# Passage to attention: next batch's adapter first, maxima over two PSUM banks, rings on released rows, value products last, squares four a tile

## The chip, the cores and the metric

One Trainium2 chip, one of its cores, one program. The metric is the device time of one execution in microseconds, lower is better. Engines: PE multiplies matrices, ACT applies functions and copies, DVE does elementwise work and reductions, POOL (GpSimd) some elementwise work, SP issues most of the DMAs. Each has its own instruction stream and they meet through semaphores.

## The reference

`x` is 8 batches of 512 rows of 256. Four layers follow each other:

- L0, a quantised GELU-gated unit: `h = x * ((cond @ norm_w.T + 1) * rsqrt(mean(x*x) + eps))`, `val, gate = split(h @ up_w.T)`, `u = val * gelu(gate)`, u rounded to 8 bits per row, times ternary `down_w`, plus x. The mean square of each row of x is needed first: these are the squares of this case.
- L1, an adapter: `x + relu(x @ Wd_b.T + bd) @ Wu_b.T + bu`, with weights of its own for each batch, generated from `cond`.
- L2: `x + alpha * attention(gamma * rmsnorm(x) + beta)`, 16 heads of 16, softmax over 512 keys, then a SwiGLU unit of width 1024 in the same form.
- L3: layer norm, plus `tanh` of a condition, times weight, plus bias.

## The kernel before, in words

**L0** runs over 32 tiles of 128 rows (n = 0 to 31; four tiles are a batch). PE multiplies each for the gate half and the value half (`up`, L1383; 12 matmuls of 512 columns each, three passes for precision), transposes the quantised rows (`transpose_q`), multiplies by the down weights (`down`) and transposes back (`transpose_x1`). ACT does `gelu`, copies qT and x1T out of PSUM, and stores rounds of generated weights (`store_round`). Its `squares(n0, n1)` (L721) sums the squares of rows with an accumulator, `roots` takes the square root, DVE the reciprocal into `r0`. For tiles 8 to 31 this is done in two blocks of 12 squares behind tiles 5 and 6 (L943 to L948).

**L1 and attention** are a pipeline of steps `step(j, ..., i)`, i = 0 to 15, one for each head, in which batch a = j + 1 is in the adapter, p = j in the query, key and value products, b = j - 1 in attention, and f = j - 2 in the output product. Each engine has its own `step`, and the order of its work is written out by hand; there is no scheduler. `opening` and the tables `ACT_PLAN`, `DVE_PLAN`, `PE_PLAN` (L52) lay the steps of j = -1 and the first of j = 0 between the last tiles of L0. What is left of j = 0 stands behind the last tile: **the passage**.

Scores are computed twice. `max_scores` (L1462) multiplies 128 queries by the 512 keys of a head into one of two PSUM banks `mx_ps`, and DVE takes the maximum of each row (`take_maxima`, L1136); 16 such columns are a group of four heads (`turn_max` transposes them, POOL splits them, SP writes them to DRAM and reads them back as two extra rows of the query ring). The scores proper, `st_ps`, then already have the maximum taken off, ACT takes the exponential, and `av_ps` gathers weights times values. Maxima run `LEAD = 7` heads ahead, so the passage holds the maxima of heads 0 to 6 of batch 0 in its steps 9 to 15, and step 0 of the round j = 1 can begin with scores of head 0 and maxima of head 7.

Queries and keys go through DRAM into `qring` and `kring`, one slot for each group of four heads (`load_ring`, L467). The slots lie on the rows of SBUF that held the up weights, so the first load waits for the last value product of L0, `val_done` of NT = 32, and for the stores of both halves of queries and keys.

PSUM is shared: the two banks of `gate_ps` are later `mx_ps`, those of `val_ps` are `st_ps0`, that of x1T is `av_ps`, that of `gen_ps` is `misc`, in which all products of the adapter, of queries, keys and values stand one after another (`take_misc` waits for its last reader). `hf` holds the normalised rows of a batch: the value products (L1552) read it, the squares of the next batch's rows are written to it (L899), and POOL then writes the next batch's rows to it (L694).

## Time and profile before

| | us |
|---|---|
| median of 3 runs | 1108.82 (1108.29 to 1127.13) |
| profiled execution | 1111.15 |
| its span | 1108.5 |
| mean granted clock of PE | 0.971 of 2.4 GHz |
| PE busy | 1042.1 (94%) |
| DVE busy | 748.0 (67%) |
| ACT busy | 664.3 (60%) |
| POOL busy | 173.8 (16%) |
| chain that ended last: PE, DVE, ACT | 69%, 12%, 6% |

PE sets the length nearly everywhere, so the rows to look for are those in which PE waits, and who released it. Times in rows are from the span's start. In a row of the timeline the bracket gives how long the engine was idle before it and what ended that. A clock of 1.00 is 2.4 GHz, of 0.50 is 1.2 GHz.

### The profile page before, as it was taken

What the parts mean: (1) busy time and instruction counts of PE and PEld (TensorE: products, weight loads), DVE (VectorE), ACT (ScalarE), POOL (GpSimd) and SP (SyncE); (2) the same over time, 40 slices, a digit from 0 to 9 for tenths busy, and PEclk for the clock granted to TensorE, in tenths of its full rate; (3) what the DMA queues carried; (4) which work ended last, traced back from release to release, by engine and by line L of the source; (5) the groups of instructions that cost most, each with busy time, mean ns of one, the idle gap of its engine ahead of it and who ended that gap; (6) DMA issues with size and microseconds to landing.
All of it is one profiled execution on the core that took longest, in us unless ns stands there. A gap on an engine that the chain in (4) does not pass through costs nothing.

```text
span 1108.5 us, 16304 instructions
## 1 busy us (share of the span) xinstructions
PE 1042.1 (94%) x5286; PEld 637.4 (57%) x5286; DVE 748.0 (67%) x1211; ACT 664.3 (60%) x903; POOL 173.8 (16%) x203
## 2 busy tenths in 40 slices
PE   6989999999789999999999999999899999999996
PEld 4756767777535344343434344333268778787784
DVE  5755667787576777777776877778855565656654
ACT  5574334463335777878787777866763555555545
POOL 0000001120131132333232432221201000000000
PEclk9999999999958999999999999999999999999998
DMA  9924422002514355353635355354220000000001
GB/s 295 385 98 138 157 94 88 1 1 86 117 30 146 72 158 117 98 142 76 200 74 163 79 158 117 99 148 106 69 59 21 1 20 20 19 19 0 20 20 38
DMA packets 63576, 103.85 MB, mean 94 GB/s; under 512 B 18720, under 2 KB 28960, under 8 KB 62496
## 3 DMA queue, kind: packets, MB, share of 16 engines
q1 hardware_dynamic: 60784, 100.56, 31.0%
q10 hardware_dynamic: 2736, 2.57, 1.0%
q8 instruction: 32, 0.52, 0.2%
q14 instruction: 24, 0.20, 0.1%
HBM read 65.81 MB, written 33.03 MB: 89 GB/s over the span
## 4 chain that ended last, share of the span: by engine, by line
PE 69%; DVE 12%; issue 7%; ACT 6%; POOL 2%; DMA 2%; SPq 1%; ACTq 0%; DVEq 0%; POOLq 0%
PE st_ps L1635 13%; PE gate_ps L1392 8%; PE val_ps L1392 8%; PE mx_ps L1635 7%; PE st_ps L1522 7%; DVE mx L1142 6%; PE av_ps L1512 6%; PE misc_ps L1448 4%; PE mx_ps L1467 3%; PE misc_ps L1539 3%; PE y_ps L1402 3%; PE misc_ps L1552 2%; PE misc_ps L1543 1%; DVE stage L1152 1%; PE qT_ps L1410 1%
## 5 line engine op out<-in xcount | busy, mean ns | idle before, releaser
L1142 DVE TENSOR_REDUCE mx<-mx_ps 128x1 f32<-128x512 f32 x512 | 330.2, 685 | 132.0 <-PE mx_ps L1467 131.8
L1467 PE MATMUL mx_ps<-kring,qring 48*128 48x512 f32 x512 | 210.8, 477 | 14.5 <-DVE mx L1142 10.9
L1522 PE MATMUL st_ps<-qring,kring 50*128 50x512 f32 x512 | 190.6, 454 | 10.0 <-ACT shared L874 4.0
L1522 PEld LDWEIGHTS st_ps<-qring,kring 50*128 50x128 f32 x512 | 79.1, 189 | 161.5 <-issue 114.6
L874 ACT ACTIVATE pbuf<-st_ps 128x1024 f32<-128x1024 f32 x128 | 129.5, 1022 | 46.5 <-PE st_ps L1522 44.1
L874 ACT ACTIVATE shared<-st_ps 128x1024 f32<-128x1024 f32 x128 | 129.1, 1024 | 41.0 <-PE st_ps L1522 39.4
L1467 PEld LDWEIGHTS mx_ps<-kring,qring 48*128 48x128 f32 x512 | 89.2, 191 | 55.4 <-DVE mx L1142 51.8
L1294 DVE TENSOR_TENSOR shared<-st_ps,shared 128x512 f32<-128x512 f32 x64 | 44.2, 690 | 80.0 <-PE st_ps L1635 61.5
L991 ACT ACTIVATE p_hi<-shared 128x512 fp32r<-128x512 f32 x64 | 40.4, 631 | 71.1 <-DVE shared L1294 70.5
L1191 DVE SCALAR_TENSOR_TENSOR h<-val_ps,r,gelu 128x1024 f32<-128x1024 f32 x32 | 41.1, 1283 | 57.3 <-PE val_ps L1392 57.3
L1303 DVE TENSOR_TENSOR p_lo<-shared,p_hi 128x512 fp32r<-128x512 f32 x64 | 46.9, 733 | 37.7 <-ACT p_hi L991 37.0
L929 ACT ACTIVATE gelu<-gate_ps,r 128x1024 f32<-128x1024 f32 x32 | 35.7, 1116 | 57.7 <-PE gate_ps L1392 57.7
L1512 PE MATMUL av_ps<-shared,vaug 128*17 128x512 f32 x512 | 68.5, 607 | 1.5 <-ACT oaug L796 1.3
L975 ACT ACTIVATE shared<-mx_ps 128x512 f32<-128x512 f32 x64 | 38.2, 597 | 51.1 <-PE mx_ps L1635 51.0
L1512 PE MATMUL av_ps<-pbuf,vaug 128*17 128x512 f32 x512 | 66.8, 598 | 1.3 <-ACT oaug L796 1.1
L766 ACT ACTIVATE qT<-qT_ps 128x1024 bf16<-128x1024 bf16 x32 | 32.6, 1017 | 54.4 <-PE qT_ps L1410 50.8
L1392 PE MATMUL gate_ps<-up_hi,xs_lo 128*128 128x512 f32 x128 | 55.0, 430 | 6.9 <-DVE up_lo L1064 6.9
L1392 PE MATMUL val_ps<-up_hi,xs_lo 128*128 128x512 f32 x128 | 54.7, 427 | 0.0
L1392 PE MATMUL gate_ps<-up_lo,xs_hi 128*128 128x512 f32 x128 | 51.8, 405 | 0.0
L1392 PE MATMUL gate_ps<-up_hi,xs_hi 128*128 128x512 f32 x128 | 51.5, 403 | 0.0
L1392 PE MATMUL val_ps<-up_hi,xs_hi 128*128 128x512 f32 x128 | 51.3, 401 | 0.0
L1392 PE MATMUL val_ps<-up_lo,xs_hi 128*128 128x512 f32 x128 | 51.1, 400 | 0.0
(223 smaller groups left out, 2087.3 us busy)
## 6 DMA issues: line engine op xcount, KB each, us to landing
chunk<-in_gen_w SPq DMA_DIRECT2D x8, 2048.0 KB, 8.8
qring<-q_parts SPq DMA_DIRECT2D x64, 192.0 KB, 3.5
kring<-k_parts SPq DMA_DIRECT2D x64, 192.0 KB, 4.5
q_parts<-stage SPq DMA_DIRECT2D x16, 512.0 KB, 2.8
k_parts<-stage SPq DMA_DIRECT2D x16, 512.0 KB, 2.8
xres<-in_xT SPq DMA_DIRECT2D x8, 512.0 KB, 12.2
shared<-in_x SPq DMA_DIRECT2D x8, 512.0 KB, 12.1
q_parts<-stage SPq DMA_DIRECT2D x16, 256.0 KB, 3.0
```

What stands on the lines that cost most here:

```text
L874: nc.scalar.activation(pbuf[g % 2][:, i % GH, 2 * half:2 * half + 2], st_ps[half][:], ACT.Exp, scale=float(DH) ** -0.5).then_inc(S["exp"], 1)
L991: nc.scalar.activation(p_hi[f % 4][:], p_f, ACT.Copy).then_inc(F["p_hi"], 1)
L1142: nc.vector.tensor_reduce(mx[h // GH % 2][:, col:col + 1], mx_ps[qt % 2][:], AX, ALU.max).then_inc(S["mx_free"], 1)
L1191: nc.vector.scalar_tensor_tensor(out=h[:], in0=val_ps[:], scalar=r0[:, bass.ds(n, 1)], in1=gelu[:], op0=ALU.mult, op1=ALU.mult) \
L1294: nc.vector.tensor_tensor(p_f, fhid_ps[f % 2], silu[f % 2], ALU.mult) \
L1303: nc.vector.tensor_tensor(p_lo[f % 4][:], p_f, p_hi[f % 4][:].bitcast(F32), ALU.subtract) \
L1392: ins = nc.tensor.matmul(ps[:, half * 512:(half + 1) * 512], a[:, k, t * P:(t + 1) * P], w[:, k, o:o + 512], start=s == 0, stop=s == len(s ...
L1448: ins = nc.tensor.matmul(out, s(k), m(k), start=n == 0, stop=n == len(steps) - 1)
L1467: nc.tensor.matmul(mx_ps[qt % 2][:], qring[r:r + QROWS, h // GH, h % GH // 2, qt * P:(qt + 1) * P], kring[r:r + QROWS, h // GH, h % GH // ...
L1512: ins = nc.tensor.matmul(av_ps[32 * c:32 * c + DH + 1, :], vaug[:, kt, GH * vg + c, :], pbuf[vg % 2][:, c, kt, :], start=kt == 0, stop=kt ...
L1522: ins = nc.tensor.matmul(st_ps[half][:, kt % 2], kring[r:r + SROWS, g, i % GH // 2, kt * P:(kt + 1) * P], qring[r:r + SROWS, g, i % GH // ...
L1635: ins = nc.tensor.matmul(out, s(k), m(k), start=first and n == 0, stop=last and n == len(steps) - 1)
```

## The change

1. Squares: four behind each of the tiles 4 to 9, with a root behind tile 7 (tiles 8 to 23) and one behind tile 10 (tiles 24 to 31).
2. Start: the second piece of up weights is loaded and copied ahead of batch 0's x and its squares.
3. Rings: `qring` and `kring` are one tensor for each group. Group 0 lies on `xs_hi0` and `xs_lo0`, which the last four tiles don't use, so its load waits for tile 27 only, and goes ahead of the last store of keys. A load waits for the stores of its own half of the heads. The extra key rows are set by eight DMAs instead of four.
4. Passage: the next batch's adapter product (step 7) first, then six heads of maxima (`first_maxima`) over two pairs of banks, `mx_ps` and `st_ps0`, with one reduction for two banks; between them the rest of L0, the adapter's up products (9, 10) and the mean square (13); the value products (5, 6) last. The squares of the adapter's result go to `vtmp` instead of `hf`.
5. Step 0 of round j = 1 takes the maxima of two heads, 6 and 7, and ACT scales `hf` there behind the exponentials instead of ahead of them, since POOL writes it only behind the value products.

PE behind the last tile (`y_ps` is the down product, `qT_ps` and `x1T_ps` the transposes, `misc_ps<-wv,hf` the value products, `misc_ps<-m_hi` the adapter's down product), before:

```order
L1402 MATMUL y_ps<-dq,qT 128x256 x8
L1552 MATMUL misc_ps<-wv,hf 128x256 x8
L1410 MATMUL qT_ps<-ident_b,q 128x128 x8
L1418 MATMUL x1T_ps<-ident,x_92 128x128 x2
L1448 MATMUL misc_ps<-m_hi,g_lo 128x512
...
L1467 MATMUL mx_ps_41<-kring,qring 128x512
L1467 MATMUL mx_ps_42<-kring,qring 128x512
```

and now, from the same place to the first attention scores, `st_ps_42<-qring_95,kring_96`:

```order
L1490 MATMUL misc_ps<-m_hi,g_lo 128x512
...
L1514 MATMUL mx_ps<-kring_96,qring_95 128x512 x2
L1514 MATMUL st_ps_42<-kring_96,qring_95 128x512 x2
L1444 MATMUL y_ps<-dq,qT 128x256 x8
L1452 MATMUL qT_ps<-ident_b,q 128x128 x8
...
L1460 MATMUL x1T_ps<-ident,x_92 128x128 x2
L1597 MATMUL misc_ps<-wv,hf 128x256 x4
L1514 MATMUL mx_ps<-kring_98,qring_97 128x512 x2
L1514 MATMUL st_ps_42<-kring_98,qring_97 128x512 x2
L1597 MATMUL misc_ps<-wv,hf 128x256 x4
L1567 MATMUL st_ps_42<-qring_95,kring_96 128x512
```

The value products moved from ahead of all maxima to both sides of the sixth head's, and the adapter's product took their place.

DVE in the same stretch (`x_92` is the residual of a tile, `xres` that of the adapter), before:

```order
L1114 SCALAR_TENSOR_TENSOR x_92<-y_ps,deq,shared 128x256
L1142 TENSOR_REDUCE mx_29<-mx_ps_41 128x1
L1142 TENSOR_REDUCE mx_29<-mx_ps_42 128x1
...
L1114 SCALAR_TENSOR_TENSOR x_92<-y_ps,deq,shared 128x256
L1142 TENSOR_REDUCE mx_29<-mx_ps_41 128x1
L1158 SCALAR_TENSOR_TENSOR xres<-misc_ps,vecs,xres 128x512
```

and now:

```order
L1138 SCALAR_TENSOR_TENSOR x_92<-y_ps,deq,shared 128x256
L1202 TENSOR_REDUCE mx_29<-mx_ps 128x2
L1202 TENSOR_REDUCE mx_29<-st_ps_42 128x2
L1183 SCALAR_TENSOR_TENSOR xres<-misc_ps,vecs,xres 128x512
...
L1156 STREAM_TRANSPOSE mT<-mx_29 128x32
L1138 SCALAR_TENSOR_TENSOR x_92<-y_ps,deq,shared 128x256
...
L1277 MEMSET av_ps 128x512
L1168 TENSOR_REDUCE mx_30<-mx_ps 128x1 x8
```

A reduction now gives two columns instead of one, the last tile's residual moved behind four heads of maxima, and the last row shows the eight maxima of step 0.

The diff, cut to its core:

```diff
+        xs_hi = [at("xs_hi0", [P, KD, L], F32R)]
+        xs_lo = [at("xs_lo0", [P, KD, L], F32R)]
...
-        qring = at("qring", [P, NG, GH // 2, L], F32R)
-        kring = at("kring", [P, NG, GH // 2, L], F32R)
+        qring, kring = [], []
+        for g in range(NG):
+            qring.append(at(f"qring{g}", [P, GH // 2, L], F32R))
+            kring.append(at(f"kring{g}", [P, GH // 2, L], F32R))
...
-        mx_ps = [pb(ctx, f"mx_ps{i}", [P, L]) for i in range(2)]
+        mx_ps = pb(ctx, "mx_ps", [P, 2, L])
...
+        wide_ps = [mx_ps, st_ps[0]]
...
+        def heads_of(j, i, has_p, has_b):
+            if isinstance(j, int) and j == 0:
+                return []
+            if isinstance(j, int) and (j, i) == (1, 0):
+                return [(0, LEAD - 1), (0, LEAD)]
+            if i + LEAD < NH:
+                return [(j - 1, i + LEAD)] if has_b else []
+            return [(j, i + LEAD - NH)] if has_p else []
...
+        def squared(j):
+            if isinstance(j, int) and j == 0:
+                return vtmp[:].rearrange("p t n -> p (t n)").rearrange("p (k t) -> p k t", k=KD)
+            return hf[:]
...
             load_up(0)
+            load_up(1)
             load_x(0)
-            for n in range(1, 4):
-                load_up(n)
+            load_up(2)
+            load_up(3)
...
-                    sp.wait_ge(A["val_done"], NT)
+                    sp.wait_ge(A["val_done"], NT if g else NT - KT)
                 else:
                     wait_apart(sp, "st_ready", 2 * (NH * (b - 1) + GH * (g + 1)), (S["raw_lo"], 3))
-                for par in range(2):
-                    sp.wait_ge(S[f"qk{par}_out"], 16 * 2 * STORES * (b + 1))
+                sp.wait_ge(S[f"qk{g * 2 // NG}_out"], 16 * 2 * STORES * (b + 1))
...
-                    for part in range(MPARTS):
-                        row = s * HALF + QROWS + part
-                        sp.dma_start(kring[row:row + 1].bitcast(F32), dens[0:HALF, :]).then_inc(S["setup"], 16)
+                    row = s * HALF + QROWS
+                    for g in range(NG):
+                        sp.dma_start(kring[g][row:row + MPARTS].bitcast(F32), dens[0:P // NG, :]) \
+                            .then_inc(S["setup"], 16)
...
+                opens = isinstance(j, int) and j == 0
+                if i == 5 and opens:
+                    load_ring(p, 0)
...
+                if isinstance(j, int) and j == 0 and i == 13:
+                    split_max(0, 0, 0)
...
+                    if isinstance(j, int) and j == 0:
+                        wait(pool, "v_ps", 2)
...
             up_high(0)
+            up_high(1)
             act.wait_ge(A["x0_loaded"], 16)
             squares(0, KT)
-            up_high(1)
             roots(0, KT)
...
+                opens = isinstance(j, int) and j == 1
+                if i == 0 and has_p and not opens:
+                    scale_rows()
...
+                if i == 0 and has_p and opens:
+                    scale_rows()
...
-                        if first and u == 5:
-                            act.wait_ge(A["x_loaded"], 16 * (NB - 2))
-                            squares(2 * KT, 5 * KT)
-                        if first and u == 6:
-                            squares(5 * KT, NT)
-                            roots(2 * KT, NT)
+                        if 4 <= n < 2 + NB:
+                            if n == 4:
+                                act.wait_ge(A["x_loaded"], 16 * (NB - 2))
+                            squares((n - 2) * KT, (n - 1) * KT)
+                        if n == 7:
+                            roots(2 * KT, 6 * KT)
+                        if n == 2 + NB:
+                            roots(6 * KT, NT)
...
-            upto(0, 6)
+            step(*flags(0), 8)
             evac_qT(NT - 1)
             evac_x1T(NT - 2, NB - 1, 2)
-            upto(0, 8)
+            step(*flags(0), 11)
+            step(*flags(0), 14)
             evac_x1T(NT - 1, NB - 1, 3)
-            upto(0, NH - 1)
+            for i in (6, 7):
+                step(*flags(0), i)
...
+            def first_maxima(h):
+                for half in range(2):
+                    wait(dve, "mx_ready", KT * h + 2 * half + 2)
+                    col = (h % 2 * (GH // 2) + h % GH // 2) * KT + 2 * half
+                    nc.vector.tensor_reduce(mx[h // GH][:, col:col + 2], wide_ps[half][:], AX, ALU.max) \
+                        .then_inc(S["mx_free"], 2)
...
-            upto(0, 9)
+            first_maxima(0)
+            step(*flags(0), 10)
+            first_maxima(1)
+            step(*flags(0), 11)
+            first_maxima(2)
+            first_maxima(3)
+            turn_max(0, 0)
             residual(NT - 1, NB - 1, 3)
-            upto(0, NH - 1)
+            first_maxima(4)
+            first_maxima(5)
...
+            def max_scores(mb, h, qt, wide=False):
                 n = KT * (NH * mb + h) + qt
-                wait(pe, "mx_free", n - 1)
                 r = h % 2 * HALF
-                nc.tensor.matmul(mx_ps[qt % 2][:], qring[r:r + QROWS, h // GH, h % GH // 2, qt * P:(qt + 1) * P],
-                                 kring[r:r + QROWS, h // GH, h % GH // 2, :], start=True, stop=True) \
+                if wide:
+                    wait(pe, "mx_free", KT * (h - 1) + qt // 2 * 2 + 2)
+                    out = wide_ps[qt // 2][:, qt % 2]
+                else:
+                    wait(pe, "mx_free", n - 1)
...
-                    pe.wait_ge(S["setup"], 16 * 2 * MPARTS)
+                    pe.wait_ge(S["setup"], 16 * 2 * NG)
                     pe.wait_ge(S["av_zeroed"], 1)
-                    pe.wait_ge(A["h"], NT)
+                    wait(pe, "mx_free", KT * (LEAD - 1))
                     pe.wait_ge(A["qT"], NT)
                     pe.wait_ge(A["x1"], NT)
...
+                        for m in range(kt * len(heads), (kt + 1) * len(heads)):
+                            max_scores(*heads[m // KT], m % KT)
...
+            def first_maxima(h):
+                if h == 0:
+                    pe.wait_ge(A["gelu"], NT)
+                    pe.wait_ge(ring[0], 64)
+                for qt in range(KT):
+                    if (h, qt) == (0, 2):
+                        pe.wait_ge(A["h"], NT)
+                    max_scores(0, h, qt, True)
+            step(*flags(0), 7)
+            first_maxima(0)
             down(NT - 2)
-            upto(0, 6)
             transpose_q(NT - 1)
             transpose_x1(NT - 2)
-            upto(0, 9)
+            step(*flags(0), 9)
+            first_maxima(1)
+            step(*flags(0), 10)
+            first_maxima(2)
             down(NT - 1)
+            first_maxima(3)
+            step(*flags(0), 13)
+            pe.wait_ge(ring[1], 64)
+            first_maxima(4)
             transpose_x1(NT - 1)
-            upto(0, NH - 1)
+            step(*flags(0), 5)
+            first_maxima(5)
+            step(*flags(0), 6)
```

## Rows read from the trace of the kernel before

**Rows 1.** The page: busy times of all engines.

```profile
PE 1042.1 (94%) x5286; PEld 637.4 (57%) x5286; DVE 748.0 (67%) x1211; ACT 664.3 (60%) x903; POOL 173.8 (16%) x203
```

**Rows 2.** Timeline at the start: start us, length us, engine, line, operation [idle before].

```profile
8.51 1.06 ACT L718 ACTIVATE up_hi<-chunk 128x1024 fp32r<-128x1024 f32 x1 [0.43 <-DMA chunk<-in_up_wT]
10.07 0.42 ACT L726 ACTIVATE sq<-shared 128x256 f32<-128x256 f32 x1 [0.50 <-DMA shared<-in_x]
14.46 0.79 PE L1392 MATMUL gate_ps<-up_hi,xs_lo 128*128 128x512 f32 x1 [0.59 <-DVE up_lo L1064]
17.18 0.69 PE L1392 MATMUL val_ps<-up_hi,xs_lo 128*128 128x512 f32 x1
```

**Rows 3.** Chain of waits in order of time: start, length, what.

```profile
57.47 3.00 PE gate_ps L1392 x12
91.98 2.94 PE gate_ps L1392 x12
```

**Rows 4.** Timeline of PE, tile 6.

```profile
72.32 1.89 PE L1402 MATMUL y_ps<-dq,qT 128*128 128x256 bf16 x8 [3.56 <-ACT qT L766]
```

**Rows 5.** Timeline of ACT, tiles 5 to 11; ACTq is its queue of DMA issues.

```profile
64.89 0.42 ACT L726 ACTIVATE sq<-shared 128x256 f32<-128x256 f32 x1 [1.85 <-issue]
71.17 0.19 ACT L726 ACTIVATION_READ_ACCUMULATOR sq<-shared 128x1 f32 x1
74.06 1.73 ACTq L783 DMA_DIRECT2D generated<-gen_out  x4
82.32 1.28 ACT L733 ACT_TABLE_LOAD   x1
113.21 3.05 ACTq L783 DMA_DIRECT2D generated<-gen_out  x4
```

**Rows 6.** Timeline of DVE in the passage.

```profile
284.49 1.22 DVE L1196 TENSOR_REDUCE amax<-h 128x1 f32<-128x1024 f32 x1
287.72 0.48 DVE L1114 SCALAR_TENSOR_TENSOR x<-y_ps,deq,shared 128x256 f32<-128x256 f32 x1
294.62 2.56 DVE L1142 TENSOR_REDUCE mx<-mx_ps 128x1 f32<-128x512 f32 x4 [6.42 <-PE mx_ps L1467]
308.20 0.74 DVE L1158 SCALAR_TENSOR_TENSOR xres<-misc_ps,vecs,xres 128x512 f32<-128x512 f32 x1
310.42 1.29 DVE L1142 TENSOR_REDUCE mx<-mx_ps 128x1 f32<-128x512 f32 x2 [0.28 <-PE mx_ps L1467]
```

**Rows 7.** Timeline of PE in the passage.

```profile
282.97 0.62 PE L1410 MATMUL qT_ps<-ident_b,q 128*128 128x128 bf16 x8
288.18 2.00 PE L1552 MATMUL misc_ps<-wv,hf 128*128 128x256 f32 x8 [0.69 <-ACT vtmp L796]
311.17 1.39 PE L1467 MATMUL mx_ps<-kring,qring 48*128 48x512 f32 x2 [0.18 <-DVE mx L1142]
315.70 2.07 PE L1578 MATMUL misc_ps<-tmp,mean_w 128*128 128x512 f32 x2
325.24 0.76 PE L1522 MATMUL st_ps<-qring,kring 50*128 50x512 f32 x1 [1.42 <-DVE av_ps L1235]
333.16 1.05 PE L1543 MATMUL misc_ps<-m_lo,wq_hi 128*128 128x512 f32 x2
```

**Rows 8.** Stretches: PE, PEld, DVE, ACT, POOL busy, clock, DMA share, GB/s.

```profile
315.00:320.00 5.00, 4.64 (x8) 1.67 (x7) 2.58 (x4) 1.32 (x2) 0.76 (x1) 0.50 0.28 67
345.00:350.00 5.00, 4.89 (x31) 2.33 (x34) 3.63 (x7) 3.42 (x5) 0.47 (x2) 1.00 0.37 148
100.24:125.10 24.86, 24.86 (x152) 17.35 (x151) 16.61 (x31) 10.09 (x14) 0.00 (x0) 1.00 0.44 145
```

**Rows 9.** Timeline of SP's issues: stores of keys.

```profile
273.04 10.18 SPq L506 DMA_DIRECT2D k_parts<-stage  x4
```

**Rows 10.** Timeline of POOL, rows of batch 1.

```profile
319.24 2.50 POOL L694 TENSOR_TENSOR hf<-xres,rn 128x512 f32<-128x512 f32 x2 [5.10 <-ACT rn L813]
329.31 2.49 POOL L638 TENSOR_TENSOR m_lo<-hf,m_hi 128x512 fp32r<-128x512 f32 x2 [6.63 <-ACT m_hi L796]
```

More of the change, by code:

```diff
@@ L1167, in step @@
                                                    op0=ALU.mult, op1=ALU.add).then_inc(S["x3"], 1)
-                take_maxima(range(early, KT))
-                if has_max(i, has_p, has_b) and split_group(i) is not None:
-                    mb, h = head_of(j, i)
-                    turn_max(NG * mb + split_group(i), split_group(i))
+                take_maxima(maxima[early:])
+                for mb, g in groups_of(heads):
+                    turn_max(NG * mb + g, g)
+            def first_maxima(h):
[4 more added lines that the diff above has]
+                        .then_inc(S["mx_free"], 2)
             upto = opening(step)
```

99 lines of the change are left out of this document (45 added, 54 removed).

## The prediction

> **What bounds the kernel now.** I read the page's totals first: PE is busy 94% of the span [rows 1], so time can only go where PE stands still, runs at the lower clock, or does less. The change leaves PE's work as it is. I then looked in the timeline of each engine for the places that the diff touches. Three stand out.
>
> *The start.* The first gate product waits for the second piece of up weights, whose ACT copy stands behind four squares [rows 2].
>
> *Tiles 5 to 8.* The chain of waits has the gate product of tile 5 at 57.47 and of tile 8 at 91.98 us [rows 3]: 34.5 for three tiles. Three undisturbed ones, from 100.24 to 125.10, take 24.9, or 8.29 each [rows 8]. The excess is **9.7 us**. The down product at 72.32 waited 3.56 us for the copy of qT [rows 4], which stood behind 12 squares on ACT. A square with its read of the accumulator costs 0.54 (12 from 64.89 to 71.36) [rows 5]; 24 of them sit behind tiles 5 and 6.
>
> *The passage.* The last tile's transposes begin at 282.97 [rows 7]. The first attention scores start at 325.24, having waited for the clearing of av_ps, and the first query product of batch 1 ends at 334.2 [rows 7]. Between them DVE took 28 maxima of 512 columns, in pairs of 1.29 with 0.28 of idle, the first at 294.62, after 6.42 us of idle [rows 6]. PE's clock was at 0.50, its lower level of 1.2 GHz, in most of this stretch [rows 8]. All of it is serial: this is the largest term.
>
> **The change, part by part.**
>
> *Squares four a tile.* The same 24 squares now follow tiles 4 to 9, 2.16 us behind each. ACT's load in an undisturbed tile: gelu and copies 3.0 (10.09 over three tiles, one of which has a further copy of 1.06 [rows 2, 8]), and four DMA issues of 1.73 to 3.05 together [rows 5]. With the squares that is 6.9 to 8.2 us against 8.29. Tiles 5 and 9 have the further copy, and behind tile 7 stands a root, whose set of functions must be loaded and then taken back: 2 × 1.28 = 2.6. The root behind tile 10 brings 2.6 again where no squares are left; the cover there is ACT's 8.3 − 4.8 = 3.5 of spare time. So the squares fit, and something spills over in tiles 4 (a copy of qT begins about 2.2 later, of which 0.8 shows), 5, 7 and 9. I take 2.0 for the spill. Bounds: none (9.7 gained) and all of it, 0.8 + 1 + 2.6 + 1 = 5.4 (4.3 gained). **Gain 7.7.**
>
> The rows show a load of 1.28 at 82.32, without idle time before it, behind the second twelve squares [rows 5]. The Trainium skill (ScalarE: Activation LUTs, "What ACT_TABLE_LOAD costs") gives every switch a drain of about 1.38 us more; by that estimate the two added switches would cost 5.3 instead of 2.6, and this gain could be 2.8 smaller. The rows show no such drain.
>
> *Start.* The second piece of up weights takes x's place in SP's queue, so ACT copies it at about 10.1, ahead of the squares, and the first gate product runs on instead of pausing 0.59 [rows 2]. But x comes one transfer later: the first piece was there at 8.51 and x at 10.07 [rows 2], so 1.5 us. Squares, root and the third piece of weights stand in this order on ACT; they begin 1.5 later, less the copy of 1.06 that was between and is now ahead: 0.5 later. The value product waits for the third piece. **Loss 0.5**; bounds: nothing if x lands sooner, 1.5 if PE's second pause keeps the clock low for longer.
>
> *Passage, up to the first attention scores.* Rings 0 and 1 no longer wait for the last store of keys nor ring 0 for the last tile: it goes out behind the third of four stores, issued from 273.04 on [rows 9], so some 9 us sooner, and is there before PE wants it. The adapter's down product takes the place of the value products. DVE is free at 288.2 (its last residual then), so its maxima begin there: 6.4 sooner than at 294.62.
>
> From there DVE's own work: 12 reductions over two banks. No row has this form; a reduction of 1024 columns from SBUF takes 1.22, a pair of 512 from PSUM 1.29 [rows 6]. I take 1.22: 14.6. Two adapter residuals of 0.74, the token residual and a small transpose, 0.7 together, and 0.5 for the clearing: 288.2 + 14.6 + 1.5 + 0.7 + 0.5 = **305.5**. Two pairs of banks let PE fill one while DVE reads the other, so the idle of 0.28 a pair goes, if PE keeps up: two score products at the low clock take 1.39 [rows 7], a little more than the 1.22 that it is to hide behind.
>
> What is late next is PE. Behind the fifth head it has the mean-square product (2.07 at the low clock), two value products (2.00 each for eight matmuls at the full clock, so some 3.6 at the low one) [rows 7], each behind a copy on ACT, and the sixth head between them. At the full clock the second value product ends at about 305.2, beside the maxima. At the low clock throughout it is 313.5. The value products are dense, and in this trace the clock came back once the dense products of batch 1's queries were in: 0.50 in 315 to 320, 1.00 in 345 to 350 [rows 8]. I take **310** for the first attention scores, 15 sooner than 325.24.
>
> *After it.* Step 0 of batch 1 holds two heads of maxima, eight reductions instead of four: +3.1 (two pairs of 1.29 + 0.28). hf is now free only after the second value product, so POOL's two products (2.50), ACT's two scalings and two copies, and POOL's two subtractions (2.49) [rows 10] stand behind it, partly beside scores and exponentials: from 310 to about 322.5 for the end of the first query product, which ended at 334.2. So of the 15, 3.3 are given back. **Gain 11.7**. Bounds: full clock, query product ends at 316 to 317 (gain 18); low clock, 327 to 329 (gain 5). Eight small SP issues instead of four for the key units stand ahead of ring 2, and ring 3 is issued behind the first rows of maxima, as before; both are wanted over 10 us later. Nothing there.
>
> *The rest.* mx_ps is one tensor of two banks; the steady rounds issue the same instructions on the same banks. The rings' new places change no wait. Nothing. Nothing in a later stage waits on an absolute time, so I expect the gain to last to the end.
>
> Sum: 1111.15 − 7.7 + 0.5 − 11.7 = 1092.3 for the profiled execution. The median of the runs is 2.3 below that execution: **1090**.
>
> **The rivals.**
>
> *Full clock in the passage* (22%). For it: the value products come in one dense stretch with little between. Against: the clock fell in the passage before and stayed at 0.50 even where PE was busy 4.6 of 5 us [rows 8]. Passage 18 instead of 11.7: **1084**.
>
> *Low clock throughout, PE the bound* (20%). For it: PE issues score products two at a time and stops between, as in the stretch that ran at 0.50. Passage 5: **1097**. The skill's rule on this (TensorE: Matmul & The Clock Gate, "A second HAM failure mode: psum-queue depth-cycling") has a kernel whose PE pauses between groups as it cycles through PSUM banks fall back to the low clock again and again. The trace before agrees for its own pauses.
>
> *ACT does not hold four squares in a tile* (8%). Every tile from 4 to 10 grows, by the bound above: 4.3 gained instead of 7.7: **1093**.
>
> *The change doesn't do what it says* (4%): the maxima start early but wait, for example for ring 0, or a step from the passage is late and the rounds of batch 1 absorb it. Only the squares gain: **1102**.
>
> *Slower* (3%). The one tensor over two banks makes DVE's reads and PE's writes in the rounds hinder each other. Place: the some 480 reductions of the rounds, about 0.65 each [rows 6], for which PE already waits. It decides from 0.04 us a reduction (480 × 0.04 = 19, the forecast gain) if all of it shows. At 0.1: 1090 + 48 = **1138**. Against: the banks were neighbours and in use at once before.
>
> **How the numbers follow.** The forecast has 43%, with 1090 and its own range of 1086 to 1094. The range to hold 8 in 10 takes in both clock cases with their bounds: 1081 (both passage and squares at their best, 1108.8 − 18 − 9.7) to 1100. About 2% (22 us) is what a measurement of this kernel can tell from no change; that line is at 1086.6. Below it lie the full-clock case, most of it, and a tenth of the forecast's own spread around it: faster 0.30, same 0.67, slower 0.03.
>
> **What the profile of the changed kernel would show.** Squares: gate products of tiles 5 to 8 every 8.3 to 9 us, no wait of y_ps for ACT over 1 us. Start: val_ps begins 0.3 to 0.7 later than 17.18. Passage: 12 reductions over two banks at 1.2 us, the first 5 us after the last tile; scores of batch 0 at 27 us after that tile's transposes instead of 42; the query product 12.5 us after the scores instead of 9. Wrong if these reductions take over 1.4, if the granted clock between is 1.00 or 0.50 throughout, if the copy of qT still holds up PE, or if a round of batches 2 to 7 is not as long as it was.

## The result, and the profile after

The changed kernel took 1095.51 us in the median of 15 runs (1086.08 to 1104.46), the kernel before 1114.48 in 15 runs beside it (1104.49 to 1128.05). The ratio is **0.9846, 95% interval 0.9801 to 0.9891**: some 17 us, or 1.5%, faster. The forecast was 1090, range 1081 to 1100. Its saving was 18.8, and 19.0 lie between the two medians; the level differs because the kernel before ran 5.7 above the median that the forecast was tied to. The ratio leaves out the slowest executions of each kernel, and the profiled one of the changed kernel is among the four left out of its 15.

The profiled execution of the changed kernel took 1102.64 (span 1099.7, mean granted clock 0.967), against 1111.15 (1108.5, 0.971) before. These two alone would say 8.5. So the places have to be read one by one, and the clock apart from them.

The page, where [rows 1] stood for the kernel before: the same work is done, in less time, so PE's share goes from 94 to 95%. The last row is the granted clock in 40 slices; it dips in slices 11 and 12 (the passage), 29 and 30 (the end of attention) and the last.

```profile
PE 1042.7 (95%) x5286; PEld 638.9 (58%) x5286; DVE 747.5 (68%) x1200; ACT 666.8 (61%) x906; POOL 174.1 (16%) x203
PEclk9999999999869999999999999999689999999998
```

**Tiles 5 to 10.** Chain of waits of the changed kernel: start, length, what. These answer to [rows 3].

```profile
67.16 2.99 PE gate_ps L1434 x12
75.47 2.99 PE gate_ps L1434 x12
100.82 2.99 PE gate_ps L1434 x12
109.12 2.99 PE gate_ps L1434 x12
```

Its timelines of PE (first two rows, against [rows 4]) and of ACT (the others, against [rows 5]), with the idle time before an instruction in brackets:

```profile
61.70 1.05 PE L1444 MATMUL y_ps<-dq,qT 128*128 128x256 bf16 x8 [0.48 <-ACT qT L781]
95.36 1.05 PE L1444 MATMUL y_ps<-dq,qT 128*128 128x256 bf16 x8 [0.29 <-ACT qT L781]
83.84 0.18 ACT L741 ACTIVATION_READ_ACCUMULATOR sq<-shared 128x1 f32 x1
84.05 1.28 ACT L748 ACT_TABLE_LOAD   x1
85.34 0.31 ACT L748 ACTIVATE rms<-ssq,eps 128x16 f32<-128x16 f32 x1
108.67 1.28 ACT L748 ACT_TABLE_LOAD   x1 [3.22 <-issue]
111.47 1.28 ACT L949 ACT_TABLE_LOAD   x1
```

The down product waits 0.48 and 0.29 for qT where it waited 3.56 and 2.83. From tile 6 to tile 7 is 8.31, an undisturbed tile. The gate product of tile 10, 108.55 in the chain before, is at 100.82.

**Start.** Timeline of PE; answers to [rows 2].

```profile
17.89 0.77 PE L1434 MATMUL val_ps<-up_hi,xs_lo 128*128 128x512 f32 x1 [2.11 <-DVE up_lo L1088]
```

The gate product does not pause any more, but the value product waits 2.11 for the third piece and starts at 17.89 instead of 17.18.

**Passage.** Timeline of DVE, against [rows 6]: twelve reductions of 1024 columns, the last four waiting for PE.

```profile
281.33 1.21 DVE L1202 TENSOR_REDUCE mx<-mx_ps 128x2 f32<-128x1024 f32 x1
290.38 1.23 DVE L1202 TENSOR_REDUCE mx<-mx_ps 128x2 f32<-128x1024 f32 x1 [0.86 <-PE mx_ps L1514]
294.38 1.22 DVE L1202 TENSOR_REDUCE mx<-mx_ps 128x2 f32<-128x1024 f32 x1 [1.04 <-PE mx_ps L1514]
299.25 1.22 DVE L1202 TENSOR_REDUCE mx<-mx_ps 128x2 f32<-128x1024 f32 x1 [2.52 <-PE mx_ps L1514]
```

Timeline of PE, against [rows 7]:

```profile
281.07 0.62 PE L1452 MATMUL qT_ps<-ident_b,q 128*128 128x128 bf16 x8 [1.48 <-DVE q L1244]
291.05 2.07 PE L1623 MATMUL misc_ps<-tmp,mean_w 128*128 128x512 f32 x2
295.54 2.94 PE L1597 MATMUL misc_ps<-wv,hf 128*128 128x256 f32 x8
302.30 0.47 PE L1567 MATMUL st_ps<-qring,kring 50*128 50x512 f32 x1 [0.77 <-DVE av_ps L1277]
313.20 1.05 PE L1588 MATMUL misc_ps<-m_lo,wq_hi 128*128 128x512 f32 x2
```

Stretches (length, then busy time of PE, PEld, DVE, ACT, POOL, the clock, DMA share, GB/s), against [rows 8]:

```profile
285.00:290.00 5.00, 4.43 (x16) 2.43 (x15) 4.51 (x5) 2.34 (x2) 1.27 (x1) 0.74 0.76 154
290.00:295.00 5.00, 5.00 (x9) 1.98 (x7) 3.55 (x5) 1.32 (x2) 0.46 (x2) 0.50 0.01 1
295.00:300.00 5.00, 5.00 (x17) 3.65 (x17) 2.48 (x3) 0.98 (x2) 0.00 (x0) 0.73 0.46 105
305.00:310.00 5.00, 4.90 (x14) 2.08 (x12) 4.38 (x9) 3.25 (x5) 0.34 (x2) 0.50 0.00 0
```

The mean-square product takes 2.07, as at 0.50 before; the first value product takes 2.94, between the 2.00 of the full clock and the low one. So PE, not DVE, ends this stretch, and the clock decides how late.

**Behind it.** The value product of batch 2 starts at 392.56 (412.44 before) and that of batch 7 at 702.72 (723.26): 310.2 between them against 310.8. The rounds kept their length, and the gain stands at 20.5 there. Then 11.7 are lost in this execution. Timeline of PE at the end of attention, changed kernel:

```profile
777.27 0.73 PE L1567 MATMUL st_ps<-qring,kring 50*128 50x512 f32 x2 [1.32 <-DMA qring<-maxima]
780.57 1.91 PE L1557 MATMUL av_ps<-shared,vaug 128*17 128x512 f32 x8
```

The same instructions in the kernel before:

```profile
797.77 0.73 PE L1522 MATMUL st_ps<-qring,kring 50*128 50x512 f32 x2 [1.28 <-DMA qring<-maxima]
798.43 1.70 PE L1512 MATMUL av_ps<-shared,vaug 128*17 128x512 f32 x8
```

and the stretches behind them, first of the changed kernel, then of the one before:

```profile
780.00:785.00 5.00, 5.00 (x17) 1.81 (x14) 5.00 (x6) 2.96 (x3) 1.28 (x1) 0.50 0.09 23
795.00:800.00 5.00, 5.00 (x16) 2.48 (x9) 2.32 (x3) 3.04 (x4) 0.31 (x1) 0.50 0.00 0
```

```profile
800.00:805.00 5.00, 5.00 (x25) 2.14 (x22) 5.00 (x6) 2.97 (x3) 1.80 (x1) 0.79 0.07 17
805.00:810.00 5.00, 5.00 (x28) 2.06 (x28) 2.75 (x5) 2.53 (x3) 0.00 (x0) 1.00 0.76 235
```

Both kernels wait 1.3 for the last rows of maxima, and both fall to 0.50 just behind that wait; the kernel before comes back after some 3 us, the changed one, with PE busy all the time, after some 24. The 21 us between them, at half speed, are by this estimate some 10 of the 11.7. The change touches nothing there.

### The profile page after: what moved, and what is told of

The parts are those of the page before. It is cut to its first block, busy times and chain, and to the rows that moved or that the text cites. A ratio compares the mean times of both kernels' runs of the same rounds, so it can differ in the third digit from the quotient of the medians.

```text
span 1099.7 us, 16298 instructions
## 1 busy us (share of the span) xinstructions
PE 1042.7 (95%) x5286; PEld 638.9 (58%) x5286; DVE 747.5 (68%) x1200; ACT 666.8 (61%) x906; POOL 174.1 (16%) x203
## 4 chain that ended last, share of the span: by engine, by line
PE 71%; DVE 13%; issue 7%; ACT 5%; POOL 2%; DMA 1%; ACTq 1%; DVEq 0%; SPq 0%; POOLq 0%
PE st_ps L1700 13%; PE val_ps L1434 8%; PE gate_ps L1434 7%; PE mx_ps L1700 7%; PE st_ps L1567 7%; PE av_ps L1557 6%; DVE mx L1168 6%; PE misc_ps L1490 4%; PE mx_ps L1514 3%; PE misc_ps L1584 3%; PE misc_ps L1597 3%; PE y_ps L1444 2%; PE misc_ps L1588 2%; DVE stage L1177 2%; PE gen_ps L1473 1%
## 5 line engine op out<-in xcount | busy, mean ns | idle before, releaser
L1168 DVE TENSOR_REDUCE mx<-mx_ps 128x1 f32<-128x512 f32 x488 | 314.8, 684 | 118.5 <-PE mx_ps L1514 117.7
L1514 PE MATMUL mx_ps<-kring,qring 48*128 48x512 f32 x500 | 201.5, 467 | 11.0 <-DVE mx L1168 7.1
L1567 PE MATMUL st_ps<-qring,kring 50*128 50x512 f32 x512 | 193.2, 458 | 9.0 <-ACT shared L892 3.6
L1514 PEld LDWEIGHTS mx_ps<-kring,qring 48*128 48x128 f32 x500 | 85.1, 188 | 45.9 <-DVE mx L1168 42.0
L1700 PE MATMUL mx_ps<-ffn_lo,gate_hi 128*128 128x512 f32 x128 | 51.3, 401 | 0.0
L1700 PE MATMUL mx_ps<-ffn_hi,gate_lo 128*128 128x512 f32 x128 | 51.3, 400 | 0.0
L1700 PE MATMUL mx_ps<-ffn_hi,gate_hi 128*128 128x512 f32 x128 | 51.2, 400 | 0.0
```

Of the source, the lines that this page charges most:

```text
L1168: nc.vector.tensor_reduce(mx[h // GH % 2][:, col:col + 1], mx_ps[:, qt % 2], AX, ALU.max).then_inc(S["mx_free"], 1)
L1514: nc.tensor.matmul(out, qring[h // GH][r:r + QROWS, h % GH // 2, qt * P:(qt + 1) * P], kring[h // GH][r:r + QROWS, h % GH // 2, :], start= ...
L1567: ins = nc.tensor.matmul(st_ps[half][:, kt % 2], kring[g][r:r + SROWS, i % GH // 2, kt * P:(kt + 1) * P], qring[g][r:r + SROWS, i % GH // ...
L1700: ins = nc.tensor.matmul(out, s(k), m(k), start=first and n == 0, stop=last and n == len(steps) - 1)
```

## The experiments

Two theories. **Work**: each part is worth what stands at its place in the traces (squares 8.5; start -0.8; passage 12.2, which is 15.2 up to the scores less 3.0 behind them), and what varies beyond that is the clock. **Interplay**: the change brings on the falls of the clock, or its parts only pay together. The yardstick of the passage is the time from the gate product of tile 31 to the first attention scores, start to start, which no earlier part enters. Each row is one profiled execution:

| kernel | tile 31 | scores | between | clock, 285 to 300 in fives |
|---|---|---|---|---|
| before | 276.58 | 325.24 | 48.7 | 1.00 1.00 0.69 |
| changed | 268.85 | 302.30 | 33.5 | 0.74 0.50 0.73 |
| e1 no passage | 269.04 | 315.51 | 46.5 | 1.00 1.00 0.57 |
| e2 squares in blocks | 277.20 | 311.77 | 34.6 | 1.00 0.91 0.50 |
| e3 x first | 267.20 | 296.82 | 29.6 | 1.00 1.00 1.00 |
| e4 one-bank maxima | 269.15 | 303.13 | 34.0 | 0.91 0.50 0.57 |
| e5 filled passage | 265.67 | 295.50 | 29.8 | 1.00 1.00 0.90 |
| e6 filled end | 268.58 | 302.11 | 33.5 | 1.00 0.65 0.50 |
| e7 values first | 269.38 | 304.30 | 34.9 | 1.00 0.82 0.50 |
| e8 rings late | 265.44 | 302.00 | 36.6 | 1.00 1.00 1.00 |
| e9 changed again | 268.97 | 305.26 | 36.3 | 0.77 0.50 0.50 |
| e10 both filled | 267.43 | 297.24 | 29.8 | 1.00 1.00 1.00 |
| e11 three filled | 268.99 | 299.51 | 30.5 | 1.00 1.00 1.00 |
| e12 the same, x first | 269.24 | 299.73 | 30.5 | 1.00 1.00 1.00 |

e1 to e4 ran on one chip, e5 to e8 on a second, e9 to e12 on a third, each beside the kernel before.

**e1, squares alone**: the kernel before with these lines of the change, and the waits and reciprocals that go with them

```diff
-                        if first and u == 5:
-                            squares(2 * KT, 5 * KT)
-                        if first and u == 6:
-                            squares(5 * KT, NT)
-                            roots(2 * KT, NT)
+                        if 4 <= n < 2 + NB:
+                            squares((n - 2) * KT, (n - 1) * KT)
+                        if n == 7:
+                            roots(2 * KT, 6 * KT)
+                        if n == 2 + NB:
+                            roots(6 * KT, NT)
```

> The kernel before with only the squares four a tile and the new start order; the passage is as before. The theory (each term is worth what the two traces show at its place: squares 8.5, start -0.8, passage 12.2) expects the gate product of tile 31 at 269.0, 7.7 sooner than before, the first attention scores 15 us behind their place in the changed kernel, at 317.5, the first query product of batch 1 at 326.5, and a time 7.7 below the kernel before. The rival that the two parts share a gain (a tile phase that starts sooner only pays because the passage is new) expects less than 4. The rival that the clock, and not the work taken off the path, makes the difference expects the time anywhere within its spread of 18 us, while the places in the trace up to 280 us still stand 7.7 sooner.

The kernel that ran does not have the new start order that this expectation names: it loads x first, as the kernel before. Measured: 1108.18 (1095.15 to 1118.51), before 1118.32; ratio 0.992 (0.987 to 0.9975), 10.1 less by the medians, 8.7 by the ratio. Tile 3 to tile 10 takes 59.13 (before 67.70), 8.6 less, and tile 31 stands at 269.04, 7.5 sooner, since tile 3 stood 1.0 later here; scores 46.5 behind it. The squares keep their gain with the old passage. The scores came 2.0 sooner than I put them: 46.5 against 48.7 with one and the same code is the first sign of how far the passage varies.

**e2, squares in two blocks**: the changed kernel with the lines above turned round.

> The changed kernel with the squares again in two blocks of twelve behind tiles 5 and 6, and one root. The theory expects the gate product of tile 10 at 109.3 instead of 100.8 (8.5 later), tile 31 8.5 later as well, and the passage unchanged from there: first attention scores 33.3 behind that gate product, as in the changed kernel. Time 8.5 above the changed kernel. Rival: the passage was short because the tile phase fed it sooner; then the scores stand more than 35 behind the gate product of tile 31.

Measured: 1107.37 (1095.90 to 1169.92), ratio to before 0.9895 (0.984 to 0.995). The time is a weak witness: five of the twelve executions lie at 1096 to 1098, six at 1106 to 1113 and one at 1169.92 with a mean clock of 0.833, and against e3's ratio of 0.983 on the same chip the squares are worth some 8 us, with intervals that overlap. The places decide. Tile 3 to tile 10 takes 67.73 (before 67.70; changed 59.20), and the passage 34.6 (changed 33.5 and, in e9, 36.3). So squares and passage add up: neither needs the other.

**e3, x first**: the changed kernel with

```diff
-            load_up(1)
             load_x(0)
+            load_up(1)
...
-            up_high(1)
             squares(0, KT)
+            up_high(1)
```

> The changed kernel with x of batch 0 again ahead of the second piece of up weights in the load queue and on ACT. The theory (the new order costs what the two traces differ by) expects the gate products of tiles 1 to 3 0.8 sooner, everything behind them as much sooner, and a time 0.8 below the changed kernel. Rival: the 0.8 between the two traces comes from the first transfers, which take longer in one execution than in another; then the gate product of tile 1 stays within 0.3 of 22.5.

Measured: 1096.91, ratio 0.983 (0.975 to 0.990), so the same as the changed kernel. Tile 1 at 20.90 and tile 3 at 40.11, 1.5 and 1.4 sooner than in the changed kernel, where the expectation had 0.8 and its rival 0.3 at most; but see e12. The finding lay elsewhere: the clock was 1.00 up to 300 here, and the passage took 29.6. Timeline of PE:

```profile
291.11 1.89 PE L1597 MATMUL misc_ps<-wv,hf 128*128 128x256 f32 x8
294.06 1.99 PE L1597 MATMUL misc_ps<-wv,hf 128*128 128x256 f32 x8
296.82 0.47 PE L1567 MATMUL st_ps<-qring,kring 50*128 50x512 f32 x1 [0.77 <-DVE av_ps L1277]
```

Nothing in the passage's code differs from the changed kernel.

**e4, one bank a reduction**:

```diff
-                    nc.vector.tensor_reduce(mx[h // GH][:, col:col + 2], wide_ps[half][:], AX, ALU.max)
+                    nc.vector.tensor_reduce(mx[h // GH][:, col:col + 1], wide_ps[qt // 2][:, qt % 2], AX, ALU.max)
```

> The changed kernel with the 12 reductions over two banks in the passage each cut into two over one bank (24 of 512 columns). The theory expects these 24 at 0.59 to 0.69 each, that is 14 to 16.5 us of DVE instead of the 13.7 of the twelve, and since TensorE, not DVE, is what the last three heads wait for (DVE was idle 0.9, 1.0 and 2.5 us behind it), at most 1 us on the first attention scores. The rival that the two-bank form is what shortened the passage expects 3 us or more there.

Measured: 1088.9 (1082.83 to 1104.99), ratio 0.974 (0.966 to 0.982), which overlaps that of the changed kernel. Timeline of DVE:

```profile
284.68 1.27 DVE L1202 TENSOR_REDUCE mx<-mx_ps 128x1 f32<-128x512 f32 x2
285.88 1.27 DVE L1202 TENSOR_REDUCE mx<-st_ps 128x1 f32<-128x512 f32 x2
```

A pair steps every 1.20, a two-bank reduction every 1.13 (284.25 to 285.38). The passage took 34.0. The wide form is worth 12 × 0.07 = 0.8 of DVE time at most, and nothing that shows; what shortened DVE's work is that PE fills two other banks meanwhile, so the idle of 0.28 a pair is gone.

**e5, filled passage**: while DVE is the one waited for,

```diff
                 for qt in range(KT):
+                    if h < 3:
+                        nc.tensor.matmul(...)
                     max_scores(0, h, qt, True)
```

> The changed kernel with each of the 12 score products of the first three heads in the passage issued twice to the same bank (12 more matmuls of 512 columns, 0.33 each at the full clock; the values are the same), where DVE, not TensorE, is what the heads wait for. The traces so far give the stretch from the gate product of tile 31 to the first attention scores as 33.5, 34.0 and 34.6 where the granted clock fell to 0.50 from about 285 on, and 29.6 in the one execution where it stayed at 1.00 up to 300. The theory (the length of the passage is decided by the clock, and the clock falls because TensorE stands still between the heads) expects 1.00 through 280 to 300, the scores 29 to 30.5 behind that gate product, and 3 to 4 less time than the changed kernel on average. Rival: the clock falls all the same, and the added matmuls cost their time at 1.2 GHz; then 34 to 37.

Measured: 1.00 to 295, passage 29.8, in spite of 12 more matmuls. All four kernels with this filling (e5, e10, e11, e12) passed in 29.8 to 30.5; of the six without it and with the changed order and rings (changed, e2, e3, e4, e6, e9) one did, the others took 33.5 to 36.3. Median 1093.36 (1085.97 to 1098.27), ratio 0.983 (0.9765 to 0.990): the 3 to 4 us that were expected don't show in the time of six runs. The clock fell to 0.50 at the end of attention in this profile too.

**e6, filled end of attention**:

```diff
+                if isinstance(j, int) and (j, i) == (NB, 3 * GH):
+                    for n in range(4):
+                        nc.tensor.matmul(mx_ps[:, n % 2], ...)
                 if has_b and i % GH == 0:
                     pe.wait_ge(mrow[i // GH], 32 * (b + 1))
```

> The changed kernel with four more score products (0.33 each) into a bank that nobody reads any more, ahead of the wait for the last rows of maxima of the last batch, where TensorE stood still for 1.32 us at 775.96 and the granted clock was then 0.50 for over 20 us (in the kernel before the same wait of 1.28 was followed by some 4 us at 0.50). The theory (that pause sets off the fall of the clock, and how long it stays down is chance) expects 1.00 throughout 760 to 820 in the profile, at most 0.2 lost to the added matmuls, and a narrower spread and a median 4 to 6 below the changed kernel. Rival: the fall comes from the light products around the pause, and the four matmuls change nothing.

Measured: 1089.31, 1086.36 to 1093.68, ratio 0.979 (0.973 to 0.985), which overlaps that of the changed kernel; the spread is 7.3, against 18.4 in the 15 runs of the changed kernel and 13.7 in the six of e9, and the granted clock 1.00 in every slice of 740 to 820. Timeline of PE:

```profile
772.99 0.85 PE L1544 MATMUL mx_ps<-kring,qring 48*128 48x512 f32 x3
774.71 0.73 PE L1572 MATMUL st_ps<-qring,kring 50*128 50x512 f32 x2 [0.88 <-DMA qring<-maxima]
```

0.88 of the wait is left, and it did not bring the clock down. In the ten profiles without this filling the clock fell there in all ten: for some 3 us in four (before, e2, e4, e9), 7 in one (e5) and 24 in five (changed, e1, e3, e7, e8), as worked out from the stretches of 760 to 830. Among the profiles that is the largest difference: 21 us more or less at 0.50, some 10 us of time. The filling is no cure every time: see e12.

**e7, values first**:

```diff
+            step(*flags(0), 5)
+            step(*flags(0), 6)
             step(*flags(0), 7)
             first_maxima(0)
...
-            if isinstance(j, int) and j == 0:
-                return vtmp[:]...
             return hf[:]
```

> The changed kernel with the value products of batch 0 ahead of the maxima again, and the squares of batch 1 in the tensor of before. The theory expects the maxima to start some 2 to 4 later and TensorE to have less behind the fourth head; since TensorE's total in the passage is the same and it is what the last heads wait for, the first attention scores come within 2 us of the changed kernel's (33.5 behind the gate product of tile 31), and the first query product of batch 1 comes 2 to 3 us sooner relative to the scores, since hf is free early. Time: within 3 of the changed kernel. Rival: the order of the value products is what made the passage short; then the scores stand 38 or more behind that gate product.

Measured: 1099.06 (1085.06 to 1109.39), ratio 0.978 (0.970 to 0.987). The first reduction is 16.5 behind tile 31 instead of 12.5, the passage 34.9; the query product ends 12.5 behind the scores, not sooner. The first half holds and the second fell. Where the value products stand is not what shortened the passage, as far as one profile tells.

**e8, rings late**:

```diff
-                    sp.wait_ge(A["val_done"], NT if g else NT - KT)
+                    sp.wait_ge(A["val_done"], NT)
...
+                    for par in range(2):
+                        sp.wait_ge(S[f"qk{par}_out"], 16 * 2 * STORES)
...
-                if i == 5 and opens:
-                    load_ring(p, 0)
```

> The changed kernel with ring 0 loaded only behind the last store of keys and the last value product of the tiles, as before. The prediction had the ring ready some 9 us sooner by the change. The theory expects the first score product of the passage to wait for the ring: in the kernel before the first maximum was 18.0 behind the gate product of tile 31, in the changed one 12.5; so the first reduction 4 to 6 later and the scores 3 to 5 later, as TensorE's other work fills a part, and 3 to 5 more time. Rival: the ring was there in time anyway, and nothing changes.

Measured: 1100.98 (1092.37 to 1112.56), ratio 0.984 (0.976 to 0.992). Timeline of PE:

```profile
280.56 1.19 PE L1516 MATMUL mx_ps<-kring,qring 48*128 48x512 f32 x2 [6.48 <-DMA kring<-k_parts]
```

PE stands 6.5 for the ring, the first reduction is 19.4 behind tile 31, and the passage takes 36.6, with the clock at 0.52 in 280 to 285 and at 1.00 from there to 305. That is 3.1 more than the changed kernel, whose clock fell, and 6.9 more than e3, whose clock did not; the first reduction too is 6.9 later. The early rings are worth 3 to 7 of the passage's 15. In the time it doesn't show: the ratio is that of the changed kernel.

**e9, the changed kernel again**

> The changed kernel once more, on the same chip as the next three. The theory (what varies in it is the granted clock, in the passage and behind the pause at the end of attention) expects a median of 1090 to 1100 and a spread of 12 us or more, with the first attention scores either 29.6 (clock kept) or 33 to 35 (clock lost) behind the gate product of tile 31, and the clock below 0.95 somewhere in 760 to 820.

Measured: 1090.71 (1088.63 to 1102.31), ratio 0.984 (0.977 to 0.991). Same code, passage 36.3 instead of 33.5. Stretches:

```profile
290.00:295.00 5.00, 5.00 (x10) 2.45 (x10) 3.10 (x5) 1.21 (x3) 0.79 (x3) 0.50 0.01 3
295.00:300.00 5.00, 5.00 (x14) 3.13 (x12) 2.36 (x2) 0.78 (x2) 0.00 (x0) 0.50 0.25 70
```

**e10, both filled**: the edits of e5 and e6.

> The doubled score products of the first three heads in the passage and the four added ones at the end of attention, in one kernel. The theory expects both effects, each as in its own run: scores 29.8 behind the gate product of tile 31, 1.00 in 760 to 820, a median of 1084 to 1089, 6 to 10 below the changed kernel, and a spread under 10. Rival (the pauses only pass the fall of the clock on to the next pause): a median within 3 of the changed kernel, and a stretch at 0.50 elsewhere, in the rounds or behind 840.

Measured: 1085.61 (1082.69 to 1089.88), 5.1 below e9 on the same chip, between the 6 to 10 that were expected and the 3 of the rival; ratio to before **0.9775 (0.9724 to 0.9825)**, whose interval overlaps that of e9. Taken together it is clearer: 17 of the 18 executions of e10, e11 and e12 took 1090.0 or less, 3 of the 6 of e9 and 2 of the 15 of the changed kernel. Stretches:

```profile
280.00:300.00 20.00, 18.75 (x76) 10.93 (x73) 18.16 (x21) 7.56 (x10) 5.11 (x6) 1.00 0.42 89
300.00:310.00 10.00, 9.64 (x25) 5.15 (x24) 6.18 (x11) 6.41 (x9) 5.52 (x10) 0.50 0.02 3
760.00:780.00 20.00, 18.29 (x99) 6.99 (x100) 18.10 (x20) 15.35 (x17) 7.28 (x4) 1.00 0.26 80
780.00:800.00 20.00, 20.00 (x104) 12.38 (x103) 10.93 (x13) 11.09 (x16) 1.71 (x1) 1.00 0.20 59
```

Both effects are there in the clock. The fall is not passed on to the end of attention, but one remains behind the scores, in 300 to 310. The last 20 us of the span, at 0.76 here, are at 0.73 to 0.83 in all 14 profiles.

**e11, three filled**:

```diff
+            for n in range(6):
+                nc.tensor.matmul(st_ps[1][:, n % 2], qring[1]..., kring[1]..., start=True, stop=True)
             for turn in iterations(pe):
```

> As the one with both, and six more score products into a bank nobody reads, between the last value product of the passage and the first attention scores, where TensorE waited 0.8 us for the clearing of av_ps, and behind it 0.8 idle again. In the run with the doubled products the clock was 0.50 from 299.5 to 315 all the same, so step 0 of batch 1 ran at 1.2 GHz. The theory expects a clock of 1.00 in 295 to 315, the first scores at most 1 later, the first query product 9 to 10 behind the scores instead of 11.6, and 2 to 4 less time. Rival: step 0's score products in pairs with pauses for DVE pull the clock down whatever stands ahead of them; then 11.6 stays and the six cost up to 1.

Measured: 1086.03 (1081.35 to 1095.46), ratio 0.975 (0.970 to 0.980), the same as e10. The clock was 1.00 to 300 and then 0.63 and 0.50; the query product ended 12.0 behind the scores. The rival holds: step 0 lost the clock with the six products ahead of it too, as in every other profile. This profile also shows the one fall in the rounds, to 0.54 in 355 to 370, behind two waits of 0.52 and 0.78 that stand at the same place in the others at 1.00.

**e12, three filled and x first**

> As the one with all three fillings, with x of batch 0 again ahead of the second piece of up weights. The gate product of tile 3 stood at 40.8 and 40.1 in the two traces with x first, and at 38.9 to 42.4 in eight with the new order. The theory that the new order costs 0.5 to 1 expects that gate product below 40.9, and a time 0.5 to 1 below the kernel before it in this list. Rival: the start varies by 3.4 us with the first transfers and the clock whatever the order, and then it can stand anywhere between 38.9 and 42.4.

Measured: 1088.98 (1086.00 to 1090.00), ratio 0.979 (0.974 to 0.984). Tile 3 at 42.16 with x first, where under 40.9 was expected. With x first (before, e1, e3, e12) the value product of tile 0 starts at 17.18 to 17.34 and tile 3 at 40.11 to 42.16, in the mean 41.2; in the ten profiles with the new order the value product starts at 17.70 to 18.07 and tile 3 at 38.95 to 42.36, in the mean 41.0. So the new order costs 0.6 at the value product, and at tile 3 nothing of it can be told from what the start varies by. At the end of attention the four products were there, with 0.87 of the wait left as in e6, and the clock fell all the same. Stretches:

```profile
775.00:780.00 5.00, 4.38 (x22) 1.37 (x22) 4.93 (x4) 4.57 (x6) 2.76 (x1) 0.77 0.01 2
780.00:785.00 5.00, 5.00 (x13) 2.61 (x10) 4.35 (x8) 1.08 (x2) 0.00 (x0) 0.54 0.24 58
```

So that filling held in three profiles of four (e6, e10, e11), where none of ten without it did; the rest of the pause is still able to bring the clock down.

## Why the prediction held, step by step

**Squares: right, the spill was half of what I took.** Tile 3 to tile 10 takes 59.2 instead of 67.7: 8.5 gained, 7.7 forecast. Seven undisturbed tiles of 8.31 would be 58.2, so 1.0 spills over: 0.6 behind the squares that follow tile 4, where the forecast had 0.8 (tile 5 takes from 58.17 to 67.09), and 0.4 behind those of tile 8, where it had none. Behind tiles 5, 7 and 9, where it had the rest, nothing spills. The root behind tile 7 with its two loads fits in the spare time. By the Trainium skill (ScalarE: Activation LUTs, "What ACT_TABLE_LOAD costs"), with its drain of about 1.38 a switch, the estimate was 2.8 less; the trace doesn't agree: the read ends at 84.02, the load starts at 84.05 and the root at 85.34.

**Start: right where it begins, not to be seen behind it.** The value product starts 0.6 later in the mean of 14 profiles, where 0.5 was forecast. The 0.7 to 0.8 between the two traces at tile 3 can't be told from chance: it varies by 3.4 there with the new order, and the two means differ by 0.2 the other way.

**Passage up to the scores: right in place and size.** Counted from a tile 31 at its old place the scores stand at 276.58 + 33.45 = 310.0; forecast 310. That is partly luck, since the number hangs on the clock: 306.2 at the full one (e3) and 312.9 at the low one (e9), where I had 305.2 and 313.5. The two reasons given are the right ones: the reductions start with the residual of the last tile but one (281.33; 288.2 less the 7.2 of the parts ahead is 281.0), and take 1.21. Early rings are a condition of it, worth 3 to 7 (e8). PE, not DVE, is late next, as the three waits of 0.9, 1.0 and 2.5 show. Two of the forecast's signs were tied to a mark that the change itself moves: the transposes of the last tile now start 12.2 behind its gate product instead of 6.4, so the first reduction stands 0.3 behind them and not 5, and the scores 21.2 and not 27.

**After the scores: right in size, by one of its two reasons.** 12.0 to the query product, 12.5 forecast, 9.0 before. The first reason, the four more maxima of step 0, is what the traces bear out. In the changed kernel the maxima behind the scores follow each other without a pause, and PE goes from the last of them to the query product without one. Timelines of DVE and PE:

```profile
303.04 5.94 DVE L1168 TENSOR_REDUCE mx<-mx_ps 128x1 f32<-128x512 f32 x8 [0.84 <-PE mx_ps L1514]
309.15 2.98 DVE L1168 TENSOR_REDUCE mx<-mx_ps 128x1 f32<-128x512 f32 x4
311.33 0.79 PE L1584 MATMUL misc_ps<-m_hi,wq_lo 128*128 128x512 f32 x1
```

From the first of step 0 to the first of step 1 are 6.1 us, where the kernel before took 3.2 for its four (326.07 to 329.23): 2.9 of the 3.0. The second reason, hf, is not on this path. POOL's products start at 301.68 behind the last value product, and its subtractions at 309.77, once ACT has made m_hi:

```profile
301.68 2.49 POOL L709 TENSOR_TENSOR hf<-xres,rn 128x512 f32<-128x512 f32 x2 [8.10 <-PE misc_ps L1597]
309.77 2.52 POOL L650 TENSOR_TENSOR m_lo<-hf,m_hi 128x512 fp32r<-128x512 f32 x2 [4.66 <-ACT m_hi L811]
```

Both copies of m_hi end at 310.22 and m_lo at 312.29, and the products that use them start at 311.33 and 313.20. And e7, with hf written by 301.33, before its scores, took 12.5 too. Nor is it the clock, which was 0.50 there (325 to 334) in the kernel before as well. No run takes the four maxima out again.

**The rest: "nothing", right in the rounds** (310.2 against 310.8), which also does away with the slower rival: a reduction takes 684 ns in the mean, 685 before. That rival had PE waiting for the reductions all through the rounds; the rows show PE idle for them 9 times before, in 345 to 765. **"I expect the gain to last to the end" failed for the profiled execution**, which took 1102.64 where the sum gave 1092.3, and held in the mean. The forecast had no step for the clock outside the passage. A line through the 45 executions of the kernel before that ran beside e1 to e12 has 8.8 us for 0.01 of mean granted clock, one through 15 of the changed kernel 9.2. At 0.975 they give 1106.4 and 1094.0: 12.4 of the gain remain at one and the same clock, and the other 5 to 6 came with a mean clock of 0.972 instead of 0.965. The passage itself can account for that. Stretch of the kernel before, then of the changed one:

```profile
285.00:345.00 60.00, 49.66 (x135) 25.67 (x133) 35.14 (x60) 20.20 (x26) 11.95 (x16) 0.66 0.37 82
285.00:345.00 60.00, 56.80 (x211) 29.83 (x209) 41.04 (x60) 32.23 (x40) 14.81 (x19) 0.77 0.39 107
```

The clock is 0.66 in both profiles with the old passage (before, e1) and 0.77 to 0.91 in six with the new one (changed, e2, e3, e4, e6, e9): in the mean some 19 us less at 0.50, which over a span of 1100 would be 0.009 of the mean clock. That is an estimate from one profile of each, not a separate test.

**The clock rivals were outcomes of one kernel, not alternatives.** I gave chances to the full and the low clock as if the code would settle it. The same code gave 33.5 and 36.3, and e3, with the same passage, 29.6. The Trainium skill (TensorE: Matmul & The Clock Gate, "A second HAM failure mode: psum-queue depth-cycling") has pauses between groups bring the clock down again and again. The fillings agree: 1.00 through 280 to 295 in four of four with them, in one of six without. The rounds speak for a limit to it: in 345 to 765 the changed kernel stayed at 1.00 with PE idle 50 times for 0.16 to 0.78 each. Only e11 fell there.

## What to carry to other kernels

Measure a part of a kernel from a landmark just ahead of it to one just behind, and in several executions, before believing a total: here two profiled totals said 8.5 us, the medians 19 and the places 20.5. Tie a forecast's sign to a mark that the change leaves where it is. Where an engine is waited for in a short transition, start its work at the earliest row that it depends on, with the loads ahead of it moved as well; the wider instruction itself was worth nothing that showed. Where TensorE stands still for about a microsecond in front of dense work, or is not the one waited for, a few more products into a bank that nobody reads cost nothing that shows here. At two places together they brought the median 5 us down on one chip, with intervals that overlap, and 17 of 18 executions to 1090.0 or less.

## What was not expected of the hardware

- One pause of 1.3 us at the same instruction was followed by some 3 us at 0.50 in one execution and by some 24 in another, with PE busy 5.00 of 5.00 in the stretches of the latter.
- At 0.50 dense matmuls of 512 columns step every 0.43 us instead of 0.23, and eight matmuls of a weighted sum take 1.91 instead of 1.05; a change in mean clock of 0.01 is 9 us here.
- A reduction over two banks steps every 1.13 us, two over one bank each every 1.20.
